# Row units of the softmax maxima over every sixteenth query of four heads, with their maxima split and loaded untransposed

## What is computed

```python
x = L0_attn_hidden_states                      # (1, 1024, 512) float32
xn = _layernorm(x, axis=-1)
# attention on xn: 32 heads of 16, 8 key/value heads, binary (sign) weights with row scales
scores = jnp.einsum('bhqd,bhkd->bhqk', q, k) / np.sqrt(HEAD_DIM)
attn = jax.nn.softmax(scores, axis=-1)
out = jnp.einsum('bhqk,bhkd->bhqd', attn, v)
...
# feed forward on xn: 512 -> 1792 -> 512, ternary weights with row scales
hidden = jax.nn.silu(gate_out) * up_out
x = x + attention + feed_forward
```

## Time and profile before

| | |
|---|---|
| median of three executions | 504.43 us (503.8 to 505.09) |
| the profiled execution, first to last instruction | 502.6 us |
| TensorE matmul busy | 479.6 us, 95% |
| VectorE busy | 417.2 us, 83% |
| ScalarE busy | 350.3 us, 70% |
| GpSimd busy | 94.4 us, 19% |
| granted TensorE clock | 1.00 over the span |

### The profile page before, as it was taken

How to read it: one execution, slowest core, us unless ns; L and a number is a source line. 1 busy time by engine, 2 the same in 40 slices (tenths; PEclk the granted TensorE clock), 3 DMA queues, 4 the chain that set the end, 5 groups by cost and what they waited for, 6 DMA issues and landing times.

```text
span 502.6 us, 10338 instructions
## 1 busy us (share of the span) xinstructions
PE 479.6 (95%) x4186; PEld 163.0 (32%) x4186; DVE 417.2 (83%) x487; ACT 350.3 (70%) x655; POOL 94.4 (19%) x138
## 2 busy tenths in 40 slices
PE   0899999999999999999999999999999999999996
PEld 0564444434332222222222222222222233333442
DVE  6879868676778999999999999999999955223986
ACT  1853643343229999999999999999999978874000
POOL 4212334534323000000000000000000113241021
PEclk9999999999999999999999999999999999999999
DMA  8862782641103802102102211111120034452321
GB/s 260 252 123 81 159 171 38 187 91 22 23 0 42 148 23 63 40 24 65 39 25 63 40 37 49 41 53 32 41 62 24 14 96 107 110 148 79 105 82 45
DMA packets 31302, 39.02 MB, mean 78 GB/s; under 512 B 6608, under 2 KB 20816, under 8 KB 31256
## 3 DMA queue, kind: packets, MB, share of 16 engines
q1 hardware_dynamic: 22232, 27.34, 19.0%
q0 software_dynamic: 8304, 10.95, 11.8%
q10 hardware_dynamic: 720, 0.08, 0.1%
HBM read 33.24 MB, written 10.35 MB: 87 GB/s over the span
## 4 chain that ended last, share of the span: by engine, by line
PE 86%; ACT 8%; DVE 3%; issue 1%; DMA 1%; SPq 0%; ACTq 0%; DVEq 0%
PE ps L1301 25%; PE ps L1131 19%; PE ps L1235 12%; PE ps L1140 8%; ACT room L705 6%; PE ps L1207 5%; PE ps L1194 5%; PE ps L1110 3%; PE ps L1335 3%; PE ps L1271 2%; ACT osb L716 1%; DMA hlo<-x 1%; DVE nmx L838 1%; PE ps L1048 1%; PE ps L1102 1%
## 5 line engine op out<-in xcount | busy, mean ns | idle before, releaser
L838 DVE TENSOR_REDUCE nmx<-ps 128x1 f32<-128x1024 f32 x248 | 284.6, 1216 | 14.5 <-PE ps L1140 14.2
L705 ACT ACTIVATE room<-ps 128x512 f32<-128x512 f32 x512 | 272.4, 598 | 20.9 <-PE ps L1271 11.0
L1301 PE MATMUL ps<-room,vcur 128*32 128x256 f32 (+1 forms) x1880 | 159.1, 410 | 4.3 <-ACT osb L716 4.1
L1140 PE MATMUL ps<-kA,qst 48*128 48x512 f16 x496 | 140.4, 382 | 0.0
L1235 PE MATMUL ps<-qst,kB 50*128 50x512 f16 x432 | 132.2, 382 | 0.8 <-DVE room L937 0.5
L1131 PE MATMUL ps<-room,wf 128*128 128x512 f16 x448 | 100.6, 379 | 0.0
L1301 PEld LDWEIGHTS ps<-room,vcur 128*32 128x32 f32 x1880 | 37.1, 108 | 100.8 <-issue 55.6
L686 ACT ACTIVATE room<-ps,gsc 128x512 f32<-128x512 f32 x28 | 19.2, 687 | 61.6 <-PE ps L1131 61.6
L1131 PEld LDWEIGHTS ps<-room,wf 128*128 128x128 f16 x448 | 42.4, 98 | 55.1 <-issue 7.2
L1235 PEld LDWEIGHTS ps<-qst,kB 50*128 50x128 f16 x432 | 26.8, 93 | 89.1 <-ACT room L705 79.8
L543 POOL TENSOR_TENSOR hlo<-room,hhi 128x512 f16<-128x512 f32 x28 | 34.1, 1217 | 87.4 <-ACT hhi L616 87.4
(11 more groups left out here) (136 smaller groups left out, 320.1 us busy)
## 6 DMA issues: line engine op xcount, KB each, us to landing
qst<-q_scratch SPq DMA_DIRECT2D x32, 192.0 KB, 3.6
o_scratch<-osb SPq DMA_DIRECT2D x16, 256.0 KB, 2.3
q_scratch<-parts SPq DMA_DIRECT2D x12, 256.0 KB
hlo<-x SPq DMA_DIRECT2D x8, 256.0 KB, 6.1
parts<-x POOLq DMA_DIRECT2D x8, 256.0 KB, 3.5
wf<-gate POOLq DMA_DIRECT2D x14, 128.0 KB, 3.9
wf<-up POOLq DMA_DIRECT2D x14, 128.0 KB, 6.0
wd<-down POOLq DMA_DIRECT2D x1, 1792.0 KB, 14.3
```

The source lines that it names most:

```text
L705: nc.scalar.activation(probs[:, s % 2, r, :], ps[:, bank_of(gp, s, i), :], ACT.Exp, scale=gam_reg[par][r]).then_inc(scores_free, 1)
L838: nc.vector.tensor_reduce(nmx[:, hf, idx:idx + 1], bank_pair(idx % 2), AX.X, ALU.max, negate=True).then_inc(rows_free, 1)
L1140: return nc.tensor.matmul(ps[:, 2 * (idx % 2) + b, :], qst[low:low + KROWS, par, hf, head, qt * P:(qt + 1) * P], kA[low:low + KROWS, par, ...
L1301: mm = nc.tensor.matmul(ps[32 * r:32 * r + 32, 7, of], vcur[:, par, key_tile(r, j), :], probs[:, s % 2, r, of], start=(j == 0 and part == ...
```

## The change

A row unit `idx` is now queries `idx`, `idx + 16`, `idx + 32`, ... of all four heads: 32 queries of each head, 128 columns of `qst`, each 16 elements (32 bytes) from the last. The maximum of head h and query 16 i + u is then at partition 32 h + i, column u, and reading `nmx[:, hf, :]` partition by partition gives exactly the order of the shift row. The transposition, ScalarE's copy and the bank entry go; GpSimd reads `nmx` itself, now with three instructions on 128 x 16; the DMA moves 128 runs of 16 float16 instead of 16 runs of 128. `split_max` waits for the last reduction of its half, and VectorE waits at a block's start until the maxima that it overwrites have been split.

```diff
-    T_AT = [n for kind, n in pe_order[:pe_order.index(("T", 0))] if kind == "F"][-1]
+    SPLIT_AT = 20
...
-    def exps_before(e):
-
-        return e - 2 if e - 3 < T_ENTRY else max(e - 3, T_ENTRY)
...
-        shp = sb("shp", [UNITS, 2, 2, P], F16)
-        mxs = sb("mxs", [UNITS, P], F32)
+        shp = sb("shp", [P, 2, 2, UNITS], F16)
+        mxs = sb("mxs", [P, UNITS], F32)
...
             def split_max(v, hf):
 
-                pool.wait_ge(max_taken, v + 1)
-                nc.gpsimd.tensor_tensor(shp[:, hf, 0, :], mxs[:, :], ones[0:UNITS, :], ALU.mult).then_inc(shift_step, 1)
-                pool.wait_ge(shift_step, v + 1)
+                pool.wait_ge(rows_free, 2 + (v + 1) * UNITS)
+                pool.wait_ge(shift_ready, v)
+                nc.gpsimd.tensor_scalar(mxs[:, :], nmx[:, hf, :], 1.0 / LIFT, 1.0, ALU.mult, ALU.mult).then_inc(shift_step, 1)
+                nc.gpsimd.tensor_scalar(shp[:, hf, 0, :], nmx[:, hf, :], 1.0 / LIFT, 1.0, ALU.mult,
+                                        ALU.mult).then_inc(shift_step, 1)
+                pool.wait_ge(shift_step, 2 * (v + 1))
                 nc.gpsimd.tensor_tensor(shp[:, hf, 1, :], mxs[:, :], shp[:, hf, 0, :], ALU.subtract).then_inc(shift_ready, 1)
...
-            def take_max(v, bank):
-
-                act.wait_ge(maxT_ready, v + 1)
-                act.wait_ge(shift_ready, v)
-                nc.scalar.activation(mxs[:, :], ps[0:UNITS, bank, 0:P], ACT.Copy, scale=1.0 / LIFT).then_inc(max_taken, 1)
...
+                if j == 0 and step < LATE:
+                    dve.wait_ge(shift_ready, ga_ * 2 + hf - 1)
...
+            def unit_queries(low, par, hf, idx):
+
+                return qst[low:low + KROWS, par, hf].rearrange("p h (i u) -> p u h i", u=UNITS)[:, idx]
+
             def half_rows(par, hf, idx, b):
 
-                head, qt = idx // (HALF // P), idx % (HALF // P)
                 low = b * HI
-                return nc.tensor.matmul(ps[:, 2 * (idx % 2) + b, :],
-                                        qst[low:low + KROWS, par, hf, head, qt * P:(qt + 1) * P],
+                return nc.tensor.matmul(ps[:, 2 * (idx % 2) + b, :], unit_queries(low, par, hf, idx),
                                         kA[low:low + KROWS, par, :], start=True, stop=True)
...
-            def transpose_max(v, hf, bank):
-                pe.wait_ge(rows_free, 2 + (v + 1) * UNITS)
-                nc.tensor.transpose(ps[0:UNITS, bank, 0:P], nmx[:, hf, :], ident[:, :]).then_inc(maxT_ready, 1)
...
-                    if w == T_AT + 1:
-                        pe.wait_ge(max_taken, 1)
...
-                    pe.wait_ge(scores_free, block_ * BLOCK + exps_before(e) + 3)
-                    if e - 3 == T_ENTRY:
-                        pe.wait_ge(max_taken, block_ + 2)
+                    pe.wait_ge(scores_free, step * REP + i + 1)
...
-                if j == T_STEP:
-                    pe.wait_ge(scores_free, block_ * BLOCK + exps_before(T_ENTRY) + 3)
-                    transpose_max(block_ + 1, 1 - hf, score_bank(T_ENTRY))
...
-                if step == ROWS_END - 1:
-                    transpose_max(2 * NG - 1, 1, LATE_T)
```

More of the change, by code:

```diff
@@ L77, in layer_kernel @@
     SUM_AT = [n for kind, n in pe_order[pe_order.index(("S", 1)):] if kind == "A"][0]
-    assert T_AT % 2 == 0 and len(PROJ) == 6
-    assert pe_order.index(("T", 0)) > pe_order.index(("A", UNITS - 1))
+    SPLIT_AT = 20
+    assert len(PROJ) == 6
+    assert dve_order.index(("F", SPLIT_AT)) > dve_order.index(("A", UNITS - 1))
     assert [n for kind, n in pe_order if kind in "FU"] == list(range(FU))
@@ L142, in fills_of, with bank_of @@
         return FILLS[done:done + QUOTAS[step - LATE]]
-    def bank_of(gp, s, i):
-        if gp * 2 * STEPS + s >= LATE:
+    def bank_of(step, i):
+        if step >= LATE:
             return LATE_SCORES[i]
-        return score_bank(entry(s % TT, i))
-    def exps_before(e):
-        return e - 2 if e - 3 < T_ENTRY else max(e - 3, T_ENTRY)
+        return score_bank(step * REP + i)
     def at(gp, s):
@@ L699, in exps @@
                 step = gp * (2 * STEPS) + s
-                if j == t_step(step // TT) + 1 and not (last and s >= STEPS + TT):
-                    take_max(gp * 4 + s // TT + 1, LATE_T if step >= LATE else score_bank(T_ENTRY))
                 act.wait_ge(probs_free, step + 1)
@@ L704, in exps @@
                     act.wait_ge(scores_ready, step * REP + i + 1)
-                    nc.scalar.activation(probs[:, s % 2, r, :], ps[:, bank_of(gp, s, i), :], ACT.Exp,
+                    nc.scalar.activation(probs[:, s % 2, r, :], ps[:, bank_of(step, i), :], ACT.Exp,
                                          scale=gam_reg[par][r]).then_inc(scores_free, 1)
@@ L1214, in scores @@
                 gp_, par, hf, j = at(gp, s)
-                block_ = gp * 4 + s // TT
+                step = gp * (2 * STEPS) + s
+                block_ = step // TT
                 if j == 0:
@@ L1228, in scores @@
                     low = half * HI
-                    e = entry(j, i)
-                    pe.wait_ge(scores_free, block_ * BLOCK + exps_before(e) + 3)
-                    if e - 3 == T_ENTRY:
-                        pe.wait_ge(max_taken, block_ + 2)
+                    pe.wait_ge(scores_free, step * REP + i + 1)
                     if opening and i == 2:
                         pe.wait_ge(h_ready, FU)
-                    nc.tensor.matmul(ps[:, score_bank(e), :],
+                    nc.tensor.matmul(ps[:, bank_of(step, i), :],
                                      kB[low:low + SROWS, par, kt % (TT // 2) * P:(kt % (TT // 2) + 1) * P],
@@ L1277, in late_scores @@
                     for b in range(2):
[L1278 to L1280 removed]
+                        mm = nc.tensor.matmul(ps[:, b, :], unit_queries(b * HI, 1, 1, unit % UNITS),
                                               kA[b * HI:b * HI + KROWS, 1, :], start=True, stop=True)
@@ L1311, in _ @@
                 for i in range(REP):
-                    last_use[bank_of(step // (2 * STEPS), step % (2 * STEPS), i)] = step * REP + i + 1
+                    last_use[bank_of(step, i)] = step * REP + i + 1
             scores(0, 0, opening=True)
```

33 lines of the change are left out of this document (5 added, 28 removed).

## The result

The changed kernel takes **511.41 us** (511.08 to 511.72, four executions) against 504.76 (503.8 to 507.82, four executions, three of which are those of the table ahead) of the one before: a ratio of 1.0122, 95% interval 1.0085 to 1.0160. It is slower by some 1.2%, where -3.6 us were forecast, and it lies outside the range of 500.2 to 509.0.

A forecast was written before the change was run, and what follows sets the result against it. TensorE and VectorE bound the loop almost equally, VectorE pausing only at each block's transposition. Terms of -3.2, -0.2 and -0.2 us, all else 0, sum to -3.6: 504.43 becomes 500.8 us, range 500.2 to 509.0.

The forecast's parts named there:

- x: Growth of a row unit's strided weight load, paid once a half step; taken as 0, gain eaten at 14 ns.
- column by column: Rival, row units' weight loads: the stride throws float16 back to the float32 way, 94 ns more, 524 us; chance 0.16.
- late steps' 8x: Late steps: the exposed growth of the row units' loads was to be paid 8 times.
- transposition in the second stage: Second stage, TensorE without idle time: removing the transposition of 0.21 us saves 0.2 us.
- Transposition in the loop: Loop, blocks 0 to 13: without transposition, ScalarE's copy and bank entry each block loses 0.23 us, together -3.2 us.
- From which VectorE's floor hides nothing: Loop: load growth adds 16x a block in full, as TensorE's 18.14 us already tops VectorE's floor of 18.13.
- exposed load: TensorE's loop: the first load of each half step is exposed, so its growth is paid 16 times a block.
- Between pairs a load is covered: TensorE's loop: loads are hidden between pairs, but not at a change between full and half rows of the array.
- GpSimd at no cost: GpSimd's split: three instructions of 0.4 us each, 1.2 us a half, hidden because the shift is needed a block later; 0.
- VectorE's new wait at no cost: VectorE, once in 16 reductions: wait for an earlier split is met on arrival; 0, at most 1.1 us.
- DMAs at no cost: Shift's DMAs: 128 runs of 32 bytes, even at 14 us, land inside the block's 18 us; cost 0.
- Half pace: Rival, row units' strided weight loads: x = 28 ns, giving 507.8 us; chance 0.25.

The follow-up runs named there:

- experiment 6: Changed kernel with another order in a loop half step: two scores, two row unit matmuls, then the value product; 506.5 us, ratio 1.0037 to the kernel before.
- experiment 1: Changed kernel with row units of 128 consecutive queries again, so without the stride, all else of the change kept; 503.72 us, ratio 0.9970.
- experiment 9: Changed kernel with a step of 2 elements and shifts loaded by 16 DMAs of 4-byte runs, last half kept at 16, last split early; 512.35 us, ratio 1.0139.

## Why the prediction was wrong

**The step that failed** is the choice of x. The 0 in the sum was my estimate, and no run shows it for a step of 16 elements: they show a load longer by 50 ns (94 to 144) and a half step longer by 0.046 (1.109 to 1.155). The other end held: the load was 144 ns, not the 192 of the float32 load, so it didn't fall to column by column. "Not column by column" and "nothing to pay" were treated as one question, and they are two: 46 ns a half step lie about midway between 0 and 94.

**The rest of the sum held in the main.** With x = 0.046 the prediction's own terms give a block of 18.14 + 16 x 0.046 = 18.88 (measured 18.80; the half step with the wait for ScalarE's copy, at a block's start, shrank from 1.50 to 1.45), 14 x (18.80 - 18.37) = 6.0 for the loop, 18 x 0.046 - 0.2 = 0.6 for the second stage, -0.2 and the new 0.8 in the late steps: 7.2 us, against 6.9 between the spans and a time of 504.43 + 7.2 = 511.6 against 511.41. The near match is partly luck, as three terms were off. The late steps' 8x, which would add 0.4, is not in this sum, for it isn't paid: a step with a row unit takes 2.61 us with either kernel (411.14 to 413.75, and 407.65 to 410.26 before), as the units stand behind four scores there, a pair like that of experiment 6. The transposition in the second stage took 4.21 - 4.10 = 0.11, not 0.2 (120.43 to 124.64 beside 124.64 to 128.74). And the count of 14 blocks was one too many: block 13 isn't longer. By the loop's first scores and the output's copies the 6.9 us divide into 0.9 up to the loop, 5.3 in blocks 0 to 12, -0.1 in block 13, 0.7 in block 14 with the wait at its end, and 0.1 behind. The part of the span before the first scores varied by up to 2.6 us among the profiled runs (151.9 to 154.6), so single spans don't size a term under 1 us.

- Transposition in the loop, -0.23 a block: right, 18.37 to 18.13 in experiment 1.
- "From which VectorE's floor hides nothing": right; half steps grew by 0.046 and VectorE went from no pause to a pace of 1.183.
- The exposed load: right in place and count in the loop, by experiment 6; the late steps' 8x contradicts the prediction's own rule, as above. "Between pairs a load is covered" holds for 144 ns too.
- GpSimd at no cost: right, 0.64 us a half. VectorE's new wait at no cost: right, experiment 1 has VectorE busy without a gap.
- DMAs at no cost: wrong for one half of 16. The cover named, a block of 18 us, wasn't there for the last half, whose rows are done only in step 3 of the block before and whose split stands behind a wait on GpSimd: from the issue at 431.63 to the time when the scores were due (440.87) it had 9.2 us. The kernel before had no more (425.70 to 434.91), and its last DMA landed 0.6 us in time. That was a check on the typical half in place of the tightest.
- **The rivals.** "Half pace" was my estimate of x = 28 ns and 507.8 us, and no run shows that term: loads grew by 17 ns at a step of 4 and by 49 and 50 at 8 and 16, and the half step by 46 at 16. It had the right kind of cause (the strided load), the right place and the right sign; its time was nearer than the forecast, and "column by column" at 524 was the other bound. The two held 0.41 together; the range cut the gap between them, where the result fell. A term that decides the sign and may be anything from 0 to 94 ns (192 - 98, the float32 and float16 loads of 128 columns in the earlier trace rows) deserved its middle as well as its ends.

## What to carry to other kernels

A rearrangement that saves an instruction by a strided operand can move the cost to whoever reads with the stride: here one transposition's 0.23 us against sixteen times 0.046 in every block. Before taking it, look for which loads are exposed (here the first behind the change from full to half rows of the array, where the pairs came 0.28 us apart instead of 0.23) and put a contiguous one there (experiment 6 got 0.49 of the block's 0.67 us back so, and paid for the order), and try smaller steps: for the float16 weights steps of 1 and 2 cost nearly the same here (94 and 95 ns), and 8 as much as 16 (143 and 144). A DMA that moves off the critical path has to be checked where its cover is thinnest, the first and the last pass, not in the steady loop.

## What was not expected of the hardware

- The 48 x 128 float16 weight load took longer with each step up to one column in 16 bytes, and 1 ns more from there to 32: 94, 95, 111, 143 and 144 ns for steps of 2, 4, 8, 16 and 32 bytes.
- Contiguous loads took longer beside strided ones: the score loads, unchanged, took 93 ns on average beside contiguous row unit loads and 105 beside strided ones, and 93 again in experiment 6, where their order puts them ahead. Whether they share a way in, and which part of it, nothing here shows.
- DMAs with 4-byte runs, 16 of them a half, cost the loop no wait where they had a block's time (blocks of 18.15, DMA engines at 0.24). Once, with 11.7 us of cover and beside a large transfer, they took 12.45 us for the issues and left a wait of 7.11 us.
- Behind the 7.11 us of idle time in experiment 9 TensorE's clock was lower, as behind the 2.07 us with a step of 8: granted 0.50 from 178 to 180 us and 0.58 on average to 184, with half steps of 2.0 and 1.7 us (value products at 180.56, 182.54 and 184.28), and 1.00 again from 184. The windows (us, PE, PEld, DVE, ACT, POOL busy, clock, DMA share, GB/s):

```profile
178.00:180.00 2.00, 0.41 (x3) 0.16 (x4) 0.00 (x0) 0.00 (x0) 0.00 (x0) 0.50 0.33 81
180.00:184.00 4.00, 4.00 (x28) 0.65 (x24) 2.45 (x2) 2.53 (x5) 0.00 (x0) 0.58 0.48 85
184.00:190.00 6.00, 5.83 (x66) 1.53 (x68) 5.73 (x5) 5.76 (x12) 0.00 (x0) 1.00 0.13 4
```
